# Two chosen experts instead of all eight: tokens sorted into 128-row tiles, in an unrolled schedule beside the recurrence

## The reference, cut to what matters

```python
xw = jnp.einsum('ntd,dh->nth', x, Wx) + b
def step(prev_h, xw_t):
    next_h = jnp.tanh(xw_t + prev_h @ Wh)          # 128 steps, one after the other
    return (next_h, next_h)
...
router_logits = jnp.einsum('bth,eh->bte', x, router_w)          # 8 experts
topk_values, topk_indices = jax.lax.top_k(router_logits, 2)
topk_weights = jax.nn.softmax(topk_values, axis=-1)
h1 = jax.nn.gelu(jnp.einsum('bth,efh->btef', x, w1) + b1, approximate=False)   # F = 512
expert_outputs = jnp.einsum('btef,ehf->bteh', h1, w2) + b2
# of the eight outputs of a token the two chosen ones are kept, weighted and summed
```

## Time and profile before

| | us |
|---|---|
| median of 3 runs (348.28 to 349.47) | 349.01 |
| the profiled execution | 348.25 |
| its span, from the first to the last instruction | 346.5 |
| DVE busy (share of the span) | 315.1 (91%) |
| PE busy | 265.4 (77%) |
| ACT busy | 213.1 (62%) |
| POOL busy | 158.3 (46%) |

### The profile page before, as it was taken

How to read it: one execution, slowest core, us unless ns; L and a number is a source line. 1 busy time by engine, 2 the same in 40 slices (tenths; PEclk the granted TensorE clock), 3 DMA queues, 4 the chain that set the end, 5 groups by cost and what they waited for, 6 DMA issues and landing times.

```text
span 346.5 us, 8439 instructions
## 1 busy us (share of the span) xinstructions
PE 265.4 (77%) x2601; PEld 190.9 (55%) x2601; DVE 315.1 (91%) x648; ACT 213.1 (62%) x427; POOL 158.3 (46%) x198
## 2 busy tenths in 40 slices
PE   5589330006698979997779999888999998776894
PEld 4434230002456867785557776556777666654673
DVE  4899999899996899799999899999889999999985
ACT  6289998160536765775447676555676665574692
POOL 1779994000086156016762109784111676639400
PEclk9989965556998998999999999999999999999999
DMA  7991443000015000000000000000001000001000
GB/s 204 332 282 38 97 86 61 0 0 0 0 33 121 2 0 0 3 2 18 0 0 0 2 23 4 0 0 0 2 0 32 0 1 0 2 3 31 0 2 23
DMA packets 28074, 12.13 MB, mean 35 GB/s; under 512 B 17369, under 2 KB 26898, under 8 KB 28050
## 3 DMA queue, kind: packets, MB, share of 16 engines
q1 hardware_dynamic: 27650, 11.63, 13.0%
q10 hardware_dynamic: 400, 0.20, 0.2%
HBM read 6.58 MB, written 1.05 MB: 22 GB/s over the span
## 4 chain that ended last, share of the span: by engine, by line
PE 39%; DVE 37%; issue 14%; POOL 3%; DVEq 2%; DMA 2%; ACT 2%; SPq 1%; ACTq 0%; POOLq 0%
PE bank L814 38%; DVE big L789 8%; DVE big L793 5%; DVE peak L562 5%; DVE wyT L749 5%; DVE big L658 2%; DVE big L668 2%; DMA x_sb<-in_x 2%; DVE big L641 2%; DVE peak L636 2%; DVE big L674 1%; DVE big L676 1%; POOL wnat L315 1%; POOL big L363 1%; ACT big L523 1%
## 5 line engine op out<-in xcount | busy, mean ns | idle before, releaser
L814 PE MATMUL bank<-wt,big 128*128 (+1 forms) x1536 | 116.3, 221 | 23.3 <-DVE big L793 14.6
L793 DVE TENSOR_TENSOR big<-big 128x384 f16<-128x384 f32 (+2 forms) x160 | 124.8, 787 | 9.5 <-ACT big L525 5.4
L814 PEld LDWEIGHTS bank<-wt,big 128*128 128x128 f16 x1536 | 97.6, 98 | 59.1 <-issue 36.2
L523 ACT ACTIVATE big<-bank,miscT 128x384 f32<-128x384 f32 (+2 forms) x160 | 96.3, 602 | 45.7 <-PE bank L814 41.3
L814 PE MATMUL bank<-big,wt 128*128 128x384 f16 (+2 forms) x480 | 110.3, 339 | 1.4 <-POOL big L363 1.4
L789 DVE CAST big<-big 128x512 f16<-128x512 f32 (+2 forms) x112 | 55.6, 497 | 7.2 <-ACT big L523 6.1
L361 POOL CAST big<-q 128x64 f16<-128x64 f32 x32 | 11.0, 344 | 98.1 <-ACT q L517 98.1
L517 ACT ACTIVATE q<-bank,miscT (+1 forms) x112 | 30.7, 274 | 39.7 <-PE bank L814 38.2
L814 PEld LDWEIGHTS bank<-big,wt 128*128 (+1 forms) x480 | 46.6, 117 | 13.7 <-POOL big L363 1.5
L814 PE MATMUL bank<-q,wxh 128*128 (+1 forms) x254 | 45.2, 254 | 2.1 <-ACT q L494 1.6
L814 PEld LDWEIGHTS bank<-q,wxh 128*128 128x128 f32 x254 | 39.1, 194 | 7.5 <-ACT q L494 3.7
(11 more groups left out here) (136 smaller groups left out, 307.6 us busy)
## 6 DMA issues: line engine op xcount, KB each, us to landing
wnat<-in_w SPq DMA_DIRECT2D x8, 512.0 KB, 7.4
x_sb<-in_x SPq DMA_DIRECT2D x4, 256.0 KB, 4.7
out_block<-wyT SPq DMA_DIRECT2D x16, 64.0 KB
b_all<-in_b SPq DMA_DIRECT2D x1, 512.0 KB, 5.5
wn<-in_w_gate ACTq DMA_DIRECT2D x1, 192.0 KB, 5.4
wn<-in_w_up SPq DMA_DIRECT2D x1, 192.0 KB, 6.0
wn<-in_w_down SPq DMA_DIRECT2D x1, 192.0 KB, 6.0
wt<-wyT SPq DMA_TRANSPOSE x8, 3.1
```

The lines of the kernel that those rows point to most:

```text
L523: A(g32[:, f, 0:w], ps_h[f][:, 0:w], ACT.Gelu, bias=bias, scale=1 / WS).then_inc(g32_done, 1)
L793: V.tensor_tensor(g_lo[:, par, f, 0:w], g32[:, f, 0:w], g_hi[:, par, f, 0:w], ALU.subtract).then_inc(g_lo_done, 1)
L814: return nc.tensor.matmul(o, l, r, start=start, stop=stop, skip_group_check=True)
```

## The change

**Which work is done.** The recurrence's tokens are taken in three spans of 512, 896 and 640 tokens. When the states of a span are there, the kernel counts on the chip how many of its tokens each expert received, and gives every token two row numbers in a list sorted by expert, in which each expert begins at a multiple of 128. POOL scatters each token's f16 pair into the two rows of a DRAM buffer `xg` (an indirect DMA for each 128-token group and choice). SP reads the buffer back with DMA transposes. Each 128-row tile of the list belongs to one expert. The number of tiles is fixed at its largest possible value, `NT` = 15, 21 and 17, so 53 tiles; the expert of each is read into registers and picks the weights' columns (`load_owners`, `w_cols`). The output of each tile goes to DRAM (`ygd`); POOL gathers the two rows of each token back (`get`), and DVE adds them with their two weights (`add_experts`). Buffers of `xg` are filled with zeros once, from SP. The biases b2 and b are added by a matmul of one row pair (`rows`) with `ones`.

**When.** Loops are gone; the order is unrolled from a table `PLAN`: for each index r (a recurrence step up to 127, a bare place in the order after) which quarters of tiles are done. A quarter is one hidden slice f of tile i and one output slice f of tile i-2 of the same span, so a span of n tiles takes n+2 units of four quarters. Span 0 is released at r = 62, with one quarter per step and a second at every third; its 68 quarters end at r = 112. Span 1 is released at r = 122, with two quarters per step. At r = 128, 156 of the 236 quarters are left (39 units); they follow at four for each r, 128 to 166. Steps below 62 have a dummy matmul of 512 columns behind them instead; steps 113 to 121 have neither.

**Small parts.** POOL splits 12 weight chunks (5 early, 7 after the first block's last step, before 11 and 3), DVE four (both halves). Chunks 8 to 15 are now written into `up2`, and the last 7 of POOL wait for the end of that buffer's use. Router logits come with the transpose of each group as 8 more columns of one f32 matmul (`turn_tokens`).

The core of the diff:

```diff
+SPANS = (512, 896, 640)
+NT = [(2 * n - E) // P + E for n in SPANS]
+UNITS = [(c, i) for c in range(NS) for i in range(NT[c] + 2)]
+RELEASE = (62, 122, 0)
+LATE = 4
-W_POOL = 14
+W_POOL = 12
+W_EARLY = 5
+def quarters():
+    plan, q = {}, 0
+    for r in range(FIRST_STEPS, T):
+        to = q
+        while to < QUARTERS and to < q + 1 + (r % 3 == 0 or r >= RELEASE[1]) and r >= RELEASE[UNITS[to // NF][0]]:
+            to += 1
+        plan[r] = (q, to)
+        q = to
+    r = T
+    while q < QUARTERS:
+        plan[r] = (q, min(q + LATE, QUARTERS))
+        q, r = plan[r][1], r + 1
+    return plan
+MIX_AT = [min(LAST_Y[0] + 22, END), min(LAST_Y[1] + 16, END), END]
+LOAD_AT = [FIRST_STEPS, RELEASE[1] - 3, T + 12]
...
+            def load_states(c):
+                sp.wait_ge(sent[c], 32 * GT[c])
+                for n in range(LOADS[c]):
+                    at = slice(4 * P * n, min(4 * P * (n + 1), P * NT[c]))
+                    sp.dma_start_transpose(hT[c][:, :, at], xg[c][at, :]).then_inc(ld_ht[c][n], 16)
...
+            link(G.tensor_scalar(rows_in[:, :], rows_in[:, :], WS, 0.0, ALU.mult, ALU.add))
+            link(G.tensor_scalar(rows[:, :], rows_in[:, :], 1.0, 0.0, ALU.mult, ALU.add))
...
+            def send(c):
+                pool.wait_ge(pos_done, c + 1)
+                pool.wait_ge(row_hi, G0[c + 1])
+                pool.wait_ge(row_lo, G0[c + 1])
+                for g in range(G0[c], G0[c + 1]):
+                    for a in range(2):
+                        G.indirect_dma_start(out=xg[c][:, :], out_offset=bass.IndirectOffsetOnAxis(ap=pos[:, a, g:g + 1], axis=0),
+                                             in_=hrow[:, g, :], in_offset=None).then_inc(sent[c], 16)
+            def get(c):
+                for m in range(4):
+                    pool.wait_ge(y_put[m], puts_before(T0[c + 1], m))
+                for g in range(G0[c], G0[c + 1]):
+                    for a in range(2):
+                        G.indirect_dma_start(out=yg[:, a, g, :], out_offset=None, in_=ygd[c][:, :],
+                                             in_offset=bass.IndirectOffsetOnAxis(ap=pos[:, a, g:g + 1], axis=0)).then_inc(got[g], 16)
...
+            send(0)
+            send(1)
+            send(2)
+            get(0)
+            get(1)
+            get(2)
...
+            def take_y(k):
+                dve.wait_ge(y_mm, k + 1)
+                if k >= 4:
+                    dve.wait_ge(y_put[k % 4], 16 * (k // 4))
+                V.tensor_copy(ysb[:, k % 4, :], ps_y[k % 2][:, 0:P]).then_inc(y_done, 1)
+            def split_gelu(k):
+                dve.wait_ge(g32_done, NF * (k + 1))
+                if k >= 3:
+                    dve.wait_ge(y_mm, k - 2)
+                V.tensor_copy(g_hi[:, k % 3, :, :], g32[:, k % 2, :, :]).then_inc(hi_v, 1)
+                dve.wait_ge(hi_v, k + 1)
+                V.tensor_tensor(g_lo[:, k % 3, :, :], g32[:, k % 2, :, :], g_hi[:, k % 3, :, :],
+                                ALU.subtract).then_inc(g_lo_done, 1)
+            def add_experts(c):
+                for g in range(G0[c], G0[c + 1]):
+                    dve.wait_ge(got[g], 32)
+                    V.scalar_tensor_tensor(acc[:, g, :], yg[:, 0, g, :], mixd[:, 2, g:g + 1], acc[:, g, :], ALU.mult,
+                                           ALU.add).then_inc(mixed, 1)
...
+            for r in range(FIRST_STEPS, END):
+                if r < T:
+                    if rnn_in(r) is not None:
+                        input_part(rnn_in(r))
+                    step(r)
+                    if r < RELEASE[0]:
+                        mm(ps_y[0][:, :], wT_hi[:, 0, :], wT_hi[:, 0:4, :].rearrange("p j o -> p (j o)"), True)
+                if r in TOKENS_AT:
+                    turn_tokens(TOKENS_AT.index(r))
+                for q in range(*PLAN[r]):
+                    if hidden_of(q):
+                        hidden(*hidden_of(q))
+                    if down_of(q):
+                        down(*down_of(q))
```

More of the change, by code:

```diff
@@ new lines, in program @@
+        upto = sb("upto", [E, E], F16)
+        seven = sb("seven", [E, 1], F16)
+        tile_no = sb("tile_no", [E, WBLK])
+        count = sb("count", [E, P])
+        tiles = sb("tiles", [E, NS, P], F16)
+        passed = sb("passed", [E, WBLK], F16)
+        owner = sb("owner", [1, NS, WBLK], I32)
+        zeros = sb("zeros", [P, 2 * P], F16)
+        xg = [nc.dram_tensor(f"xg{c}", [NT[c] * P, 2 * P], F16, kind="Internal").ap() for c in range(NS)]
+        ygd = [nc.dram_tensor(f"ygd{c}", [NT[c] * P, P], F32, kind="Internal").ap() for c in range(NS)]
@@ L294, in _ @@
+            for c in range(NS):
+                if MIX_AT[c] == END:
+                    put_out(c)
+            sp.wait_ge(stored, 16 * NG)
         @block.gpsimd
@@ L477, in _ @@
                     take_xT(n + 1)
-            for i in range(W_POOL, W_CHUNKS):
-                weight_hi(i)
             def low_byte(c):
@@ L486, in _, with step @@
                 low_byte(c)
[L487 to L490 removed]
+            def step(r):
                 act.wait_ge(rnn_mm, r + 1)
[L493 to L498 removed]
+                A(h32[:, r * B:(r + 1) * B], state(r), ACT.Tanh, scale=1 / WS).then_inc(h32_done, 1)
@@ L811, in _ @@
+            for c in range(NS):
+                if MIX_AT[c] == END:
+                    add_experts(c)
         @block.tensor
@@ new lines, in rank_tokens @@
+            def rank_tokens(c):
+                n = GT[c]
+                if c == 0:
+                    pe.wait_ge(routing, 1)
+                pe.wait_ge(row_lo, G0[c + 1])
+                pe.wait_ge(picked_done, c + 1)
+                flat = picked[:, G0[c]:G0[c + 1], :].rearrange("p j e -> p (j e)")
+                mm(ps_route[:, 0:n * E], below[:, :], flat, True)
+                for d in range(1, n):
+                    mm(ps_route[:, d * E:n * E], ones[:, 0:P], flat[:, 0:(n - d) * E], False)
+                for j in range(n):
+                    last = mm(ps_route[0:E, P:2 * P], picked[:, G0[c] + j, :], ones[:, 0:P], False)
+                last.then_inc(rank_mm, 1)
@@ new lines, in hidden @@
+            def hidden(c, i, k, f):
+                if f == 0:
+                    pe.wait_ge(ld_ht[c][i // 4], 16)
+                n = NF * k + f
+                if n >= 3:
+                    pe.wait_ge(g32_done, n - 2)
+                o = ps_h[n % 3][:, 0:P]
+                hi, lo = (hT[c][:, a, P * i:P * (i + 1)] for a in range(2))
+                w_hi, w_lo = (w_cols(owners[c][i], f, 0, low) for low in range(2))
+                mm(o, w_hi, hi, True)
+                mm(o, w_hi, lo, False)
+                mm(o, w_lo, hi, False).then_inc(hid_mm, 1)
@@ new lines, in down @@
+            def down(c, i, k, f):
+                o = ps_y[k % 2][:, 0:P]
+                if f == 0:
+                    pe.wait_ge(g_lo_done, k + 1)
+                    if k >= 2:
+                        pe.wait_ge(y_done, k - 1)
+                    mm(o, ones[0:LO_ROW + 1, 0:P], rows[:, bass.ds(owners[c][i] * P, P)], True)
+                hi, lo = (g[:, k % 3, f, :] for g in (g_hi, g_lo))
+                w_hi, w_lo = (w_cols(owners[c][i], f, 1, low) for low in range(2))
+                mm(o, hi, w_hi, False)
+                mm(o, hi, w_lo, False)
+                last = mm(o, lo, w_hi, False)
+                if f == NF - 1:
+                    last.then_inc(y_mm, 1)
```

599 lines of the change are left out of this document (290 added, 309 removed).

## The result

| | before | after |
|---|---|---|
| median | 348.65 us (348.28 to 349.47) | 365.55 us (363.61 to 367.14) |
| ratio | | 1.048 (95% interval 1.041 to 1.055) |
| profiled execution / span | 348.25 / 346.5 | 364.04 / 362.3 |
| DVE busy | 315.1 | 200.2 |
| PE busy | 265.4 | 256.2 |

A forecast was written before the change was run, and what follows sets the result against it. DVE, with PE close behind, was taken to bound the experts' part. Start 108.0, recurrence end 204.5, standstill to 236.5, units to 291.2, tail to 313.4, plus 1.75 outside: 315 us forecast, range 287 to 346.

The forecast's parts named there:

- the size of a unit: Tiles behind the recurrence: 39 units at 1.5 us each, ends 1.39 and 1.9.
- the +6 there: Stretch from recurrence's end to span 0's last gather: row numbers 8 us behind the end, landing at 236.5; measured 6 longer.
- the standstill: Behind the recurrence DVE waits for span 0's gathers, queued on POOL behind span 2's scatters: some 20 us, only POOL working.
- the 22: Stretch from span 0's last gather to the last output copied, forecast 236.5 to 291.2; measured 22 us longer.
- the 9.7 us in r = 62 to 112: Excess over the forecast for 51 steps with 68 quarters: 42.7 us, plus 2.0 for input parts and token groups.
- 0.76 and 0.84 for a recurrence step: Recurrence: 0.76 us a step from r = 16 to 61, about 0.84 in the mean to 112.
- the 10.8 us: Excess over the forecast for steps 16 to 61: 46 x 0.76 = 35.0 us plus 1.5, r = 62 at 144.5.
- Rival C: Recurrence and tiles: small pieces don't pack or dummies don't hold the clock; steps 0.9, units 1.9, together 344 us; 13%.
- The indirect DMA, taken at 1.23: POOL's scatters and gathers: each indirect DMA issue takes 1.23 us of POOL.
- Rivals A and B: POOL's indirect DMAs: cheap at 0.41 us, total 292 (25% with Rival D); or dear at 2.2, total 361 (12%).
- Rival D: Behind the recurrence: no standstill, as gathers don't wait as thought; 315 - 20 = 295 us; 25% together with the cheap-DMA rival.
- The tail: After the last output copy: trip to DRAM, ten gathers, an addition and stores, from 291.2 to the span's end at 313.4.

The follow-up runs named there:

- the first experiment: Changed kernel with the experts' weight columns picked by constants instead of registers, so no owner loads or address instructions: 340.45 us, ratio 0.976.
- the combined kernel: Changed kernel with span 0's gathers before span 2's scatters, two dummies below step 62 and in steps 114 to 121, merged output matmuls: 322.62 us, ratio 0.927.

## Why the prediction was wrong, by its own steps

**The failed step: the size of a unit.** "I take 1.5; the ends are 1.39 and 1.9, where half of the address work shows." It is 2.44. I had both numbers in hand: 25 matmuls of 0.056 are 1.39, and the 16 address instructions of 46 ns are 0.74, together 2.13 (there are 17 in a unit, 901 for 53 tiles, with the one of the bias row). In the kernel before that work was free because two address instructions stood beside three matmuls of 256 to 512 columns or nine of 128. Now they stand beside three of 128, and as the first experiment shows three matmuls and their two addresses take 0.25 instead of 0.167, that is (0.25 - 0.167) x 8 = 0.67 us for a unit; the other 0.17 of the 0.84 that it took off are not in this product, and no run tells them apart. (With constants DVE is the bound, so 0.84 is what shows, not the whole price.) The upper end should have been the whole sum and more. I had "hidden in the slots of before" as my reason, and named the thing that hides it (wider matmuls), which the change takes away.

Span 2's row numbers reach POOL at 239.9, 13.9 us behind the recurrence's end and not 8, and that is the +6 there. Of the 32 units behind the standstill 26 are whole, 26 x 0.94 = 24 us more; the six at the ends of spans have half the work, and those whose copies show it took 1.3 to 1.9, near the 1.5 charged. Span 1's additions, 3.6 us in the sum, now hide for the most part beside PE; that comes to some 21 of the 22.

Of the 9.7 us in r = 62 to 112 the register work is the smaller part. With constants the stretch took 50.6 us for 54.5, so 3.9 of them: 1.5 are the load of owners at r = 62 (2.39 for 0.88), which the sum put at nothing, 3.6 the address work in steps 76 to 112, less some 1.2 because steps 70 to 75 were still at half clock in that run. The rest stays without it: steps 63 to 69 run at half clock and take 10.75 us, with constants 10.6, where the quarters alone were forecast at 6.0 and one input part lies in them (3.20 us at r = 68).

**The second failed step: 0.76 and 0.84 for a recurrence step.** In fact two errors of opposite sign. At full clock a step is 0.67 and not 0.76, since the tanh takes 184 ns now. It has lost its operand `miscT` (the bias, which a matmul adds). First the kernel before, then the changed one:

```profile
L494 ACT ACTIVATE q<-bank,miscT x16: 258/274/275, 94.0 to 106.4; 128x16 f32<-128x16 f32 x16
```

```profile
L585 ACT ACTIVATE q<-bank 128x16 f32<-128x16 f32 x128 | 23.5, 184 | 68.8 <-PE bank L916 68.6
```

That is 90 ns, and the step is 90 shorter too. The Trainium skill (ScalarE: Activation LUTs, "What ACT_TABLE_LOAD costs") gives 93 ns for each per-partition pointer operand of an ACTIVATE; the trace agrees, with 90. But the step stayed at 0.67 for only seven steps (r = 16 to 22) and then took 0.88. The rest of the 10.8 us is the wait for `topi`, 3 to 4, which the prediction didn't have at all (DVE now splits four weight chunks by itself and is through with them only at 113), and input parts and transposes at half speed. Rival C had this mechanism, at 13%, and its evidence was in the profile: PE's clock at half through 52 to 78 us. Rival C priced a step at 0.9, measured 0.88, and the units at 1.9, measured 2.44; with the units at 2.44 its sum (344, though its terms add up to 345) is 344 + 39 x 0.54 = 365. That this is the measured time is partly luck (it had 14 us for the recurrence, where 21 were lost, and more than the 28 behind it), but the mechanism was named, and the range missed because the units' upper bound was too low.

**What held.** The indirect DMA, taken at 1.23 from the DMA transposes, starts every 1.26 us. Three scatters of span 2 and the first gather in POOL's timeline of the changed kernel:

```profile
239.88 0.96 POOL L478 DMA_INDIRECT xg<-big,pos  x1 [30.35 <-DVE pos L849]
...
250.04 0.96 POOL L478 DMA_INDIRECT xg<-big,pos  x1 [0.30 <-issue]
251.31 0.96 POOL L478 DMA_INDIRECT xg<-big,pos  x1 [0.30 <-issue]
252.57 0.99 POOL L487 DMA_INDIRECT wnat<-ygd,pos  x1 [0.30 <-issue]
```

Rivals A and B, which hung on 0.41 and 2.2, are out. The Trainium skill's DMA: Bandwidth & Descriptors, "Anatomy of one DMA — SWDGE (gpsimd) path", calls descriptor generation small; here it differs, with 0.96 us of POOL for each DMA of 128 rows, and the measurement decides. Span 1's gathers, which the prediction's row would have made 1.7 us each beside DVE's casts, started 1.24 to 1.42 us apart. The standstill came where it was said and as long as it was said; its waits, in the changed kernel (us in total, times, longest):

```profile
PE bank L916 <- DVE big L870: 20.9, 3, 19.1
...
DVE wyT L880 <- DMA wnat<-ygd,pos: 33.3, 9, 12.7
```

PE waits 19.1 us for a split by DVE, which stands behind four additions that each wait for their gathers, the first for 12.7. Rival D is out by the same rows, and the experiment with the gathers first shows the cause. The tail: 22.2 forecast, 21.7 measured, with PE and ACT at nothing, POOL's gathers and DVE's additions behind them. The bare steps 113 to 121 took 7.0 for 6.9, by luck: four of 0.67, one of 0.78 and four of 0.88 for nine of 0.76. PE's three loads of owners took 1.37 to 1.77 us each, for the 1 assumed of the later two:

```profile
L271 PEldq TENSOR_LOAD <-owner x3: 1369/1647/1772, 152.9 to 293.9; - x3
```

The check on the whole is the kernel without register work, with the gathers first and two dummies. It ran in 311.0, where the prediction less its standstill of 20 gives 295. Of the 16 us between, 9 lie in the recurrence (r = 127 at 213.2 for about 204): the wait for `topi`, and steps such as r = 63 with 2.07 us, in which PE waits 1.27 for ACT's gelu, and r = 68 with 3.15, an input part and two quarters at half clock. Some 3 more are units of 1.60 for 1.5; the last 3 or so are not traced to a cause.

## What to carry to other kernels

Work that is hidden is hidden by something: when a change makes matmuls narrower, price every address and wait instruction that stands between them in full, because the cover can go with the columns. Count whole and half units apart. When sorting cuts the work by more than half, the bound moves from throughput to chains (the recurrence at whatever clock it gets, one queue of indirect DMAs), so write down each queue's order and ask of every gather what stands ahead of it. A dummy that is meant to hold a clock has to be read in the granted clock, not argued from the room it fits in. And check a price read from three steps against the whole stretch: 0.5 us for each three steps would be 8 in all, the run without register work gave back 3.9.

## What the runs showed of the hardware that I had not expected

Two address instructions of 46 ns between three 128-column matmuls cost 0.08 us a group at the full clock, 0.25 for 0.167, and nothing at half, 0.32 for 0.32. A load of owners (15 to 21 registers) from SBUF holds PE's queue for 1.4 to 1.8 us, longest for the 15. A 128x16 tanh of the recurrence takes 184 ns, and its step 0.67 us where it was 0.76. With the later transposes the granted clock fell to 1.2 GHz five steps after a dummy of 0.38 us had been put into every step of 0.67, and PE was then busy for 38.04 of 39 us without getting the higher level back; with two dummies, in the combined kernel, it stood at 1.00. A recurrence step is only 0.21 us longer at half clock, 0.88 for 0.67.
